# Router dot products and step-size terms moved to TensorE, two more input products a batch to GpSimd

## What is computed

```
xh = layernorm(x)                                  # per token, no gain
rank, B, C = split(xh @ x_proj_w.T, [64, 16, 16])
delta = softplus(rank @ dt_proj_w.T + dt_b)        # 512 channels
h[t]  = exp(delta[t] * A) * h[t-1] + delta[t] * B[t] * xh[t]   # 512 x 16 states
y[t]  = (h[t] * C[t]).sum(states) + xh[t] * D
x1    = x + y
weights = layernorm(x1) @ router_w + router_b      # one number per token
out   = layernorm(x1) + x1, except for the 127 tokens of highest weight in
        each sequence, which go through attention and MLP times their weight
```

## Time and profile before

| | |
|---|---|
| median of the runs | 4458.69 us |
| the profiled execution | 4463.26 us, span 4461.5 us |
| scan phase | from the start to about 3451 us |
| busy, of the span | VectorE 3768.9 us (84%), GpSimd 3363.5 (75%), TensorE 3066.8 (69%), ScalarE 2861.0 (64%) |
| granted TensorE clock | 0.756 in the mean |

### The profile page before, as it was taken

One profiled execution on the slowest core, in us unless ns is written; L12 is line 12 of the kernel. 1 busy time (PEld: TensorE's weight loads), 2 busy tenths in 40 slices (PEclk: granted clock), 3 DMA queues, 4 the chain that ended last, 5 costly groups with the idle time before them and its releaser, 6 DMA issues. The chain is left out here.

```text
span 4461.5 us, 61468 instructions
## 1 busy us (share of the span) xinstructions
PE 3066.8 (69%) x17574; PEld 1408.3 (32%) x17574; DVE 3768.9 (84%) x3027; ACT 2861.0 (64%) x4425; POOL 3363.5 (75%) x1716
## 2 busy tenths in 40 slices
PE   4667665766676666665665756666664289999997
PEld 1222232322232222222232323222222145555553
DVE  2999999999999999999999999999998754555552
ACT  5777777777778687868777777777774223332221
POOL 3999999999999999999999999999998100000010
PEclk7767676767766676667676767676775589999998
DMA  4454546463646455554545464636453300000000
GB/s 102 104 136 121 148 114 158 96 170 87 171 101 156 114 144 130 127 136 122 134 123 135 124 152 105 164 84 180 92 146 76 144 22 20 19 19 19 19 19 8
DMA packets 198219, 472.94 MB, mean 106 GB/s; under 512 B 60688, under 2 KB 61200, under 8 KB 197088
## 3 DMA queue, kind: packets, MB, share of 16 engines
q1 hardware_dynamic: 177136, 452.11, 40.3%
q0 software_dynamic: 20736, 16.88, 1.4%
HBM read 126.83 MB, written 73.43 MB: 45 GB/s over the span
## 5 line engine op out<-in xcount | busy, mean ns | idle before, releaser
L955 POOL TENSOR_TENSOR ch<-hid,cmat 128x1024 f32<-128x1024 f32 x1024 | 2385.4, 2358 | 92.7 <-DVE hid L821 76.4
L821 DVE TENSOR_TENSOR_SCAN hid<-place,inp 128x1024 f32<-128x1024 f32 x1024 | 2266.1, 2270 | 105.4 <-ACT place L671 87.3
L671 ACT ACTIVATE place<-delr,a_neg 128x1024 f32<-128x1024 f32 x1024 | 1126.8, 1111 | 293.6 <-DVE hid L821 190.2
L444 PE MATMUL ps_y<-ch,nsum 128*32 128x256 f32 x8192 | 856.5, 517 | 424.3 <-POOL ch L955 423.4
L810 DVE TENSOR_TENSOR inp<-place,bmat 128x1024 f32<-128x1024 f32 x816 | 941.6, 1211 | 64.2 <-ACT place L677 63.4
L455 PE MATMUL ps_y<-ident,ysb 128*128 128x128 f32 x1024 | 319.2, 408 | 599.0 <-ACT ysb L684 580.0
L444 PEld LDWEIGHTS ps_y<-ch,nsum 128*32 128x32 f32 x8192 | 254.6, 137 | 1025.6 <-POOL ch L955 753.2
L917 POOL TENSOR_TENSOR inp<-dxr,bmat 128x1024 f32<-128x1024 f32 x208 | 490.2, 2357 | 0.0
L455 PEld LDWEIGHTS ps_y<-ident,ysb 128*128 128x128 f32 x1024 | 230.5, 278 | 807.9 <-ACT ysb L684 759.1
L1216 POOL DMA_INDIRECT out_rows<-row,idx_out x16 | 41.1, 2571 | 532.3 <-issue 298.4
L439 PE MATMUL ps_y<-xhT,dskip 128*32 128x256 f32 x2048 | 260.8, 600 | 134.2 <-ACT xr L691 134.2
(11 more groups left out here) (176 smaller groups left out, 4202.8 us busy)
## 6 DMA issues: line engine op xcount, KB each, us to landing
dxr<-dxT SPq DMA_DIRECT2D x1024, 128.0 KB, 2.4
delr<-delT SPq DMA_DIRECT2D x1024, 128.0 KB, 2.4
xr<-in_x SPq DMA_DIRECT2D x32, 1024.0 KB, 6.6
bmat<-b_and_c SPq DMA_DIRECT2D x256, 128.0 KB, 3.4
cmat<-b_and_c SPq DMA_DIRECT2D x256, 128.0 KB, 3.1
x_rows<-xr SPq DMA_DIRECT2D x16, 2048.0 KB, 7.7
out_rows<-xr SPq DMA_DIRECT2D x32, 1024.0 KB, 5.1
w<-in_w SPq DMA_DIRECT2D x2, 4096.0 KB, 24.4
```

What stands on the lines that cost most here:

```text
L444: last = pe.matmul(ps_y[q * CH:(q + 1) * CH, 0:2 * P], nsum[:], ch[:, g, q * 2 * P:(q + 1) * 2 * P], start=False, stop=(g == GROUPS - 1))
L671: nc.scalar.activation(place[:, PLACE[par, c, g], :], delr[:, c % 2, :], ACT.Exp, scale=a_neg[:, i:i + 1])\
L821: nc.vector.tensor_tensor_scan(hid[:, g, :], place[:, PLACE[par, c, g], :], inp[:, g, :], 0.0, ALU.mult, ALU.add).then_inc(hid_ready, 1)
L955: nc.gpsimd.tensor_tensor(ch[:, g, :], hid[:, g, :], cmat[:, g, :], ALU.mult).then_inc(ch_ready, 1)
```

## The change

- TensorE adds the four terms for k = 0 and 1 too, and ScalarE copies the sums; GpSimd keeps one step per block, `make_dx`. The tables for z, logarithms, pairs of terms and copies are new: k = 2's z moves from chunk 15 of the batch before to chunk 2, its logarithms from chunk 0 to chunks 2 and 3; k = 3's z from chunk 4 to 5, its logarithms from chunk 5 to 5 and 6; k = 1 goes one to two chunks later.
- The router's dot product is split into that of x and that of y. For x, the projection's weights get 32 more columns, all the router's weights, and eight matmuls turn one row of the result to tokens. For y, `ysb` keeps all 16 chunks, and 32 matmuls (2 blocks x 16 chunks) with four columns each sum it, behind group (0,0) of the next batch. ScalarE copies both results; GpSimd scales and adds them in 3 + 5 small steps. VectorE has no part in it any more.
- `OWN_AT` goes to chunk 15: GpSimd makes 15 input products a batch instead of 13.
- GpSimd writes `hid * C` over `hid`; the buffer `ch` is gone, and the scan of (c,g) waits for TensorE's sum of (c-1,g).

```diff
-Z = (12, 13, 15)
-Z3 = 4
-DELTA = {(13, 0): (1, 0, 0), (13, 1): (1, 0, 1), (13, 2): (1, 0, 2), (13, 3): (1, 0, 3),
-         (14, 3): (1, 1, 0), (15, 0): (1, 1, 1), (15, 2): (1, 1, 2), (1, 0): (0, 1, 3),
-         (2, 3): (0, 2, 3), (7, 3): (0, 3, 3)}
-ADD_TERMS = {(2, 0): ((0, 2), (0, 3), (1, 1)), (2, 1): ((1, 1), (1, 2), (2, 1)),
-             (3, 0): ((5, 2), (5, 3), (6, 1)), (3, 1): ((6, 1), (6, 2), (7, 1))}
-LOG = {(12, 3): (1, 0, (0, 1, 2)), (14, 0): (1, 1, (0,)), (14, 1): (1, 1, (1,)), (14, 2): (1, 1, (2,)),
-       (0, 0): (0, 2, (0,)), (0, 1): (0, 2, (1,)), (0, 2): (0, 2, (2,)),
-       (5, 0): (0, 3, (0,)), (5, 1): (0, 3, (1,)), (5, 2): (0, 3, (2,))}
-RW_COPY = (2, 1)
-ROUTER = (2, 3)
+Z_PE = {(11, 3): (1, 0, 0), (12, 0): (1, 0, 1), (14, 2): (1, 1, 0), (14, 3): (1, 1, 1),
+        (1, 3): (0, 2, 0), (2, 0): (0, 2, 1), (4, 3): (0, 3, 0), (5, 0): (0, 3, 1)}
+Z_ACT = {(12, 1): (1, 0, 0), (12, 2): (1, 0, 1), (14, 3): (1, 1, 0), (15, 1): (1, 1, 1),
+         (2, 1): (0, 2, 0), (2, 2): (0, 2, 1), (5, 1): (0, 3, 0), (5, 2): (0, 3, 1)}
+LOG = {(12, 3): (1, 0, (0, 1, 2)), (15, 2): (1, 1, (0,)), (15, 3): (1, 1, (1,)), (0, 1): (0, 1, (2,)),
+       (2, 3): (0, 2, (0,)), (3, 0): (0, 2, (1,)), (3, 1): (0, 2, (2,)),
+       (5, 3): (0, 3, (0,)), (6, 0): (0, 3, (1,)), (6, 1): (0, 3, (2,))}
+TERMS_PE = {(13, 0): ((1, 0, 0, 0),), (13, 1): ((1, 0, 0, 1),), (13, 3): ((1, 0, 1, 0),), (14, 0): ((1, 0, 1, 1),),
+            (0, 2): ((0, 1, 0, 0),), (0, 3): ((0, 1, 0, 1),), (1, 1): ((0, 1, 1, 0),), (1, 2): ((0, 1, 1, 1),),
+            (3, 1): ((0, 2, 0, 0),), (3, 2): ((0, 2, 0, 1),), (4, 1): ((0, 2, 1, 0),), (4, 2): ((0, 2, 1, 1),),
+            (6, 1): ((0, 3, 0, 0), (0, 3, 0, 1)), (6, 3): ((0, 3, 1, 0), (0, 3, 1, 1))}
+COPY_STEP = {(13, 3): (1, 0, 0), (14, 2): (1, 0, 1), (1, 1): (0, 1, 0), (1, 3): (0, 1, 1),
+             (4, 1): (0, 2, 0), (4, 3): (0, 2, 1), (6, 3): (0, 3, 0), (7, 1): (0, 3, 1)}
+DELTA = {(14, 2): (1, 0), (2, 0): (0, 1), (5, 0): (0, 2), (7, 2): (0, 3)}
+ROUTE_Y = ((0, 0), (0, 0))
+COPY_ROUTE_Y = (0, 2)
+ROUTE_X = (15, 1)
+COPY_ROUTE_X = (15, 3)
+SCALE_ROUTE_X = (0, 2)
-OWN_AT = tuple(range(1, 14))
+OWN_AT = tuple(range(1, 16))
...
# TensorE
-                    last = pe.matmul(aux[0:R + 2 * N, :], xproj[:, k, :],
+                    last = pe.matmul(aux[:], xproj[:, k, :],
...
+            def router_x(b):
+                aux_free(b, ("route_x",))
+                for t in range(TC):
+                    last = pe.matmul(aux[:, t:t + 1], xpT[R + 2 * N:P, t * P:(t + 1) * P],
+                                     ident[R + 2 * N:P, R + 2 * N:R + 2 * N + 1], start=True, stop=True)
+                last.then_inc(aux_full, 1)
+            def router_y(b, t, emptied):
+                if t == 0:
+                    pe.wait_ge(aux_emptied, emptied)
+                for c in range(CHUNKS):
+                    last = pe.matmul(aux[:, 4 * t:4 * t + 4], ysb[:, c, t * P:(t + 1) * P], rw_chunk[:, c, :],
+                                     start=(c == 0), stop=(c == CHUNKS - 1))
+                if t == 1:
+                    last.then_inc(route_y_full, 1)
...
-                                     ch[:, g, q * 2 * P:(q + 1) * 2 * P],
+                                     hid[:, g, q * 2 * P:(q + 1) * 2 * P],
...
# ScalarE
+            def copy_router_y(b):
+                if has(b, 1):
+                    act.wait_ge(wcol_ready, b)
+                act.wait_ge(route_y_full, b + 1)
+                nc.scalar.activation(route_y[:].rearrange("p (q t) -> p t q", t=2),
+                                     aux[:, 0:TC].rearrange("p (t q) -> p t q", t=2), ACT.Copy)\
+                    .then_inc(route_y_copied, 1)
...
# VectorE
-                    dve.wait_ge(ch_ready, tile(b, c, g) - GROUPS + 1)
+                    dve.wait_ge(ch_summed, tile(b, c, g) - GROUPS + 1)
...
-                    if has(b, 1) and c in ROUTER:
-                        router(b - 1, other, ROUTER.index(c))
...
# GpSimd
+            def make_dx(b, par, k):
+                pool.wait_ge(aux_emptied, b * NUSE + USE["s", k, 1] + 1)
+                i, j = xhat_slot(k, par)
+                nc.gpsimd.tensor_tensor(dxT[:, k, :], delT[:, k, :], xhT[:, i, j, :], ALU.mult).then_inc(dx_made[k], 1)
...
-                        nc.gpsimd.tensor_tensor(ch[:, g, :], hid[:, g, :], cmat[:, g, :],
+                        nc.gpsimd.tensor_tensor(hid[:, g, :], hid[:, g, :], cmat[:, g, :],
```

More of the change, by code:

```diff
@@ L423, in add_terms @@
                     aux_free(b, ("s", k, h))
+                    if (k, h) == (1, 0) and has(b, 1):
+                        pe.wait_ge(route_y_copied, b)
                     pe.wait_ge(z_act, b * KD * ZACT + k * ZACT + ZACT)
@@ L463, in _ @@
                 project(0, 0, h)
-            for k in range(3):
+            for k in range(2):
                 for h in range(2):
                     step_size(0, k, h)
+                if k == 1:
+                    router_x(0)
+                else:
+                    for h in range(2):
+                        for first in (True, False):
+                            add_terms(0, k, h, first)
             pe.wait_ge(dskip_ready, KD)
@@ L477, in body @@
                         sum_states(b, par, c, g)
[L479 to L489, removed]
+                        if (c, g) in Z_PE:
+                            ahead, k, h = Z_PE[c, g]
+                            if not (ahead and final):
+                                step_size(b + ahead, k, h)
+                        if (c, g) == ROUTE_Y[0] and has(b, 1):
+                            for t in range(2):
+                                router_y(b - 1, t, b * NUSE + USE["route_x",] + 1)
+                        if (c, g) == ROUTE_X and not final:
+                            router_x(b + 1)
+                        for ahead, k, h, part in TERMS_PE.get((c, g), ()):
+                            if not (ahead and final):
+                                add_terms(b + ahead, k, h, part == 0)
                         if final:
@@ L712, in _ @@
                 copy_proj(0, h)
[L713 to L721 removed]
+            for h in range(2):
+                z_half(0, 0, h)
+            exp_log(0, 0)
+            for h in range(2):
+                copy_step(0, 0, h)
+            for h in range(2):
+                z_half(0, 1, h)
+            copy_dx(0, 0, 0)
+            for g in range(2):
+                exp_decay(0, 0, 0, g)
+            exp_log(0, 1, (0, 1))
+            copy_router_x(0)
             def beside(b, par, c, place):
                 at = (c, place)
[L726 to L734 removed]
+                for ahead, k, h in (Z_ACT[at],) if at in Z_ACT else ():
+                    if not (ahead and is_last(b)):
+                        z_half(b + ahead, k, h)
+                for ahead, k, parts in (LOG[at],) if at in LOG else ():
+                    if not (ahead and is_last(b)):
+                        exp_log(b + ahead, k, parts)
+                for ahead, k, h in (COPY_STEP[at],) if at in COPY_STEP else ():
+                    if not (ahead and is_last(b)):
+                        copy_step(b + ahead, k, h)
                 if has(b, 1):
@@ L864, in _ @@
             batches(dve, body)
-            last = nb_run - 1
-            for h in range(2):
-                router(last, 1, h)
             dve.wait_ge(wt_ready, 1)
@@ L972, in _ @@
             ln1_finish(0)
-            for k, steps in ((0, 4), (1, 3)):
-                for step in range(steps):
-                    delta(0, 0, k, step)
+            make_dx(0, 0, 0)
             batches(pool, body)
             ln2_finish(nb_run - 1)
-            route(nb_run - 1)
+            route(nb_run - 1, 1)
     return out_done
```

190 lines of the change are left out of this document (90 added, 100 removed).

## The result

The changed kernel takes 4782.4 us (median of four, 4766.7 to 4797.5) against 4457.6: a ratio of 1.073, interval 1.069 to 1.076. It is slower by 7.3%, where the forecast was 4447.

The account below looks back on a forecast made before the run. VectorE and GpSimd are nearly full, VectorE waiting mostly for ScalarE's `place`. A middle batch of 195.05 + 0.7 + 2.8 + 4.1 + 7.2 + 0.3 = 210.2 us against 211.4 gave 4447, range 4375 to 4520.

Parts of the forecast that it names:

- the price of a pass: TensorE's dot product with y: 0.105 us a pass at clock 0.50, or half of that.
- the lump: TensorE's 64 passes for y behind sum (0,0): 3.4 to 6.7 us, costing VectorE 2.8 us a batch.
- the sum: Adding up a middle batch: 210.2 us against 211.4, -17 over 14 batches; with first, last and end, -12.
- the seam: Where two batches meet: old waits of some 4 us go; the loop's turn, 0.7 a batch, stays.
- the part on TensorE's dot products: x: 16 passes in chunk 15, 1.7 us, hidden; y: 64 passes behind sum (0,0), 3.4 to 6.7 us.
- the lump decides: Slower rival, chance 0.15: y's passes cost above 0.12 us; at 0.16 the time is 4515, at 0.21 4570.
- ScalarE's moved logarithms: VectorE waits for ScalarE's bursts: 4.1 us a batch in chunks 2 to 4, 7.2 in chunks 6 and 7.
- The working by gaps: ScalarE's side work above its gaps, 6.4 us a chunk, eats 3.1 us of slack, then VectorE waits.
- The new wait for the sum: Scan (c+1,g) waits for TensorE's sum of (c,g): taken as 0; as rival 1 to 2 us a batch, chance 0.1.
- Once: Start and end of the kernel: first make_dx 5.7 us later, net +1.4; end +6.3 at half clock.
- The cover holds: Faster rival, chance 0.25: y's passes at full clock, ScalarE on time into chunk 2, no z wait; about 4365.

Follow-up runs that it names:

- the pieces: Changed kernel with block k=0 hurried and all 32 matmuls of y's dot product spread behind sums (15,1) to (0,0): 4635.4 us.
- The four edits: Each alone against the changed kernel: 30 of 32 y matmuls left out, 4606.3 us; block k=0 hurried, 4726.1; logarithms cut for k=2, 4713.6, for k=3, 4750.0.
- the last one: Kernel with ScalarE's side work spread and the y product's operands changed over, its places worked out once more: 4409.7 us, ratio 0.989 against the kernel before.

## Why the prediction was wrong, step by step

It failed at two steps: the price of a pass of the lump with y, and a wait that the sum put at nothing, that for B behind a moved step. The rest roughly held. VectorE's idle times in its timeline, added up by chunk (us a batch, mean of the 14 middle batches), beside the terms of the sum:

| where | forecast | measured |
|---|---|---|
| the seam, to the end of chunk 0 | 0.7 | 7.6 |
| chunk 1 (the lump) | 2.8 | 10.9 |
| chunks 2 to 4 | 4.1 | 6.1 |
| chunk 5 | 0 | 0.8 |
| chunks 6 and 7 | 7.2 | 8.8 |
| chunks 13 and 14 | 0.3 | 1.4 |
| all | 15.1 | 35.6 |

Of the 20.5 us that the sum lacked, 15.0 stand in the first two rows.

*The price of a pass* (the part on TensorE's dot products). The forecast took 3.4 to 6.7 us for the lump, from four passes with 16 streamed columns and from ten loads at full clock. The lump took 13.8, 0.215 a pass. Both rows were of another kind: they are `pe.transpose` in the kernel (L1267 and L1334), which shows one record, where a float32 matmul shows two. And no row showed that 0.105 halves at full clock. Right behind the first of them, still at 0.50, the trace of before has float32 matmuls with 128 weight columns:

```profile
3539.75 7.17 PE L1272 MATMUL ps_s<-rows_f,gT 16*128 16x128 f32 x32
```

That is 0.22 a pass, and 14 us for 64 of them: the lump's price, there to be read before the run. By the pieces, a 128-column load with four columns behind it costs 0.12 at 1.00 and 0.22 at 0.50, so even at full clock the lump is 7.7, outside the range. The rival "the lump decides" had the mechanism and the price: it gave 4570 at 0.21, which is 123 over the forecast. Taking out the lump gave 176, where the forecast had 2.8 a batch, 45 in all, for it: 131. Its chance, 0.15, was the error; the seam's clock of 0.50 spoke for it and was named.

Under that step a rule of the Trainium skill was weighed: "TensorE: Matmul & The Clock Gate", in the section on LDWEIGHTS, prices a load by its columns alone and names no clock for it; 128 columns are by it an estimated 107 ns. The trace agrees with it at 1.00 only roughly and not at 0.50: the same loads fill 0.12 us a pass in the one and 0.22 in the other.

*The queue behind a moved step.* The sum has no term for what a later `make_dx` does at the seam: the copies of dx for the next batch wait for it in SyncE's queue, and the 16 copies of B stand behind them. That cost VectorE 94.8 us of waits, 6.3 at each of the 15 seams, none of it in the sum or in a rival. Hurrying `make_dx` by some 7 us removed all of it (56 us of time net).

*ScalarE's moved logarithms.* Chunk 3 was forecast at 1.7 and 1.75; the timeline has 1.72 and 1.73, in the next batch 2.27 and 1.73. Chunk 4: 0.5 and 0.62. Chunks 6 and 7: 3.05, 1.3 and 2.9; measured 3.92, 1.61 and 2.51, in the next batch 5.25, 1.16 and 2.86. The working by gaps was right, a little low in chunk 6. What adds there is open; ScalarE's waits for x by DMA were 7.4 us in all 16 batches, too few to carry it. The experiments with cut logarithms say what they are worth in time: 69 and 32 us.

*The new wait for the sum.* Taken at 0; 11.2 us in all, 0.7 a batch. That rival falls, and with it the in-place product as a cause. What TensorE's sums do cost stands on ScalarE: its copies of the step size waited 197 us for the sums of the four terms, mostly in chunks 5 and 14. What VectorE pays of that was not tried by itself; its waits in chunks 5, 13 and 14 are 2.2 us a batch, where the sum had 0.3.

*Once.* The start was forecast 5.7 later for `make_dx`; the first scan is 6.7 later. The end was forecast at +6.3 and is +12.8: the last lump again.

*The sum.* The excess of the changed kernel over the kernel before is 322 us (4782.4 - 4460). The four edits taken alone give 176 + 56 + 69 + 32 = 333. That this comes near is luck: what two of them leave out, logarithms, the kernel before does too, and the 56 is net of what came back. "The cover holds" fell at its first condition, the lump at full clock. The scans' 314.5 us close by VectorE's own rows: its waits grew by 426 us (535 from 109) and its busy time shrank by 114 (3768.9 to 3654.7, by the two pages), which makes 312. The forecast's 195.05 for 203.6 would have been some 131 less work, 8.55 in 15 batches and 2.3 in the first, which did no router sums before; each stop gives some 0.1 of it back, since a scan alone takes 2.29 where its pace in a row is 2.185.

## What to carry to other kernels

Before moving work to an idle engine, price it at the clock that engine has at that place, from a row of the same kind and shape (a matmul's, not a transpose's); if there is none, take the dear end as the likeliest. Ask of each step made later what stands behind it in the same DMA queue, to the last copy, not only of its own copies. And an engine that is freed gains nothing while another one meters its buffers out: here the savings came only in the runs that spread ScalarE's bursts, changed the lump's operands over and moved block k=0 ahead all at once. The spreading alone, with the lump in pieces, still took 4560.3.

## What the runs showed of the hardware

- A float32 pass with 128 weight columns and 4 streamed ones takes 0.12 us at a granted clock of 1.00 and 0.22 at 0.50, with loads filling the time in both.
- TensorE was busy for all of the 13.8 us of the lump, and the granted clock stayed at 0.50; the lump with operands changed over, 256 columns streamed in each pass, had a mean clock of 0.77 to 1.00 in the same place. Behind a first narrow piece that ran at 1.00 the clock was 0.50 for the next.
- Swapping the operands left the time of a pass about the same (0.226 at 1.00 for 0.215 at 0.50) and halved their number.
- VectorE's stop at a loop's turn ("issue") is 1.46 us before, up to 3.1 in the changed kernel and up to 4.7 in the last one; with block k=0 hurried it is as good as gone (0.3 in all). What sets it was not tried.
